# A two-layer graph kernel: tile 1 decoded by VectorE, GpSimd's work in other forms, the clip of the norm moved

## What is computed

```python
def _ngcf_conv(x, W1, W2, src, dst, n_nodes):
    deg_out = jnp.clip(segment_sum(ones, src), 1.0)
    deg_in = jnp.clip(segment_sum(ones, dst), 1.0)
    norm = jax.lax.rsqrt(deg_out[src] * deg_in[dst])
    h_src = x[src]
    h_dst = x[dst]
    msg = (h_src @ W1 + h_src * h_dst @ W2) * norm[:, None]
    agg = jax.ops.segment_sum(msg, dst, num_segments=n_nodes)
    return x @ W1 + agg

h = jnp.maximum(_layernorm(x, axis=-1), 0.0)
h = relu(_ngcf_conv(h, W1_1, W2_1, src, dst, n))
h = _ngcf_conv(h, W1_2, W2_2, src, dst, n)
return x + h
```

## Time and profile before

| | |
|---|---|
| median of three runs | 563.75 us (563.54 to 563.83) |
| the profiled execution | 563.75 us, of which the span is 559.7 us |
| PE, DVE busy in the span | 493.3 us (88%), 423.7 us (76%) |
| ACT, POOL busy in the span | 247.3 us (44%), 192.4 us (34%) |

### The profile page before, as it was taken

One profiled execution on the slowest core, in us unless ns is written; L12 is line 12 of the kernel. 1 busy time (PEld: TensorE's weight loads), 2 busy tenths in 40 slices (PEclk: granted clock), 3 DMA queues, 4 the chain that ended last, 5 costly groups with the idle time before them and its releaser, 6 DMA issues.

```text
span 559.7 us, 19159 instructions
## 1 busy us (share of the span) xinstructions
PE 493.3 (88%) x7774; PEld 457.8 (82%) x7774; DVE 423.7 (76%) x1157; ACT 247.3 (44%) x661; POOL 192.4 (34%) x307
## 2 busy tenths in 40 slices
PE   0294688899797999599999999999999999999995
PEld 0073577687586877499999999999899999999995
DVE  4698469999888798777887787788766666767673
ACT  0285488899796888523223222322211111111111
POOL 3679698879999998400000000000000000000000
PEclk9998699999989799889999999999999999999999
DMA  2166110000000000000000000000000020002011
GB/s 69 52 102 113 53 30 19 7 19 3 19 3 20 2 21 2 1 2 3 3 2 2 4 2 2 2 4 2 3 1 2 4 40 2 3 2 39 3 26 18
DMA packets 19428, 9.87 MB, mean 18 GB/s; under 512 B 16081, under 2 KB 18657, under 8 KB 19342
## 3 DMA queue, kind: packets, MB, share of 16 engines
q1 hardware_dynamic: 18222, 5.93, 5.9%
q0 software_dynamic: 1120, 2.72, 1.9%
HBM read 5.19 MB, written 1.65 MB: 12 GB/s over the span
## 4 chain that ended last, share of the span: by engine, by line
PE 35%; DVE 22%; POOL 12%; issue 10%; ACT 6%; SPq 2%; DMA 1%; DVEq 0%; ACTq 0%; POOLq 0%
PE diff L789 25%; DVE mixed L583 8%; PE slab L737 5%; ACT h L870 2%; POOL hist L394 2%; DVE work L667 2%; PE diff L773 2%; SPq L344 2%; DVE work L645 2%; PE diff L720 2%; DVE work L651 2%; DVE work L654 2%; POOL h L454 2%; POOL words L397 2%; DVE los L547 2%
## 5 line engine op out<-in xcount | busy, mean ns | idle before, releaser
L547 DVE TENSOR_TENSOR los<-mixed,iota_bank 128x6144 bf16<-128x6144 bf16 x49 | 161.9, 3344 | 10.9 <-PE slab L737 10.9
L789 PE MATMUL diff<-los,mixed 128*128 128x129 f16 x2401 | 159.7, 222 | 6.3 <-DVE los L626 5.7
L789 PEld LDWEIGHTS diff<-los,mixed 128*128 128x128 fp8e4 x2401 | 153.4, 101 | 8.3 <-issue 5.8
L789 PE MATMUL diff<-late,mixed 128*128 128x128 f16 x2401 | 150.7, 219 | 1.1 <-DVE late L670 1.1
L789 PEld LDWEIGHTS diff<-late,mixed 128*128 128x128 fp8e4 x2401 | 145.6, 98 | 2.0 <-DVE late L670 0.7
L737 PEld LDWEIGHTS slab<-hots,los 128*128 128x128 bf16 x2352 | 123.8, 101 | 22.0 <-ACT saved L831 8.4
L737 PE MATMUL slab<-hots,los 128*128 128x98 fp8e5 x2352 | 130.6, 213 | 4.6 <-DVE los L547 4.4
L823 ACT ACTIVATE hots<-diff 128x784 f16<-128x784 f32 x147 | 118.0, 843 | 18.7 <-PE diff L720 18.6
L720 PE MATMUL diff<-select,mixed 80*128 80x392 f16 x294 | 70.7, 345 | 30.3 <-DMA mixed<-rows 18.0
L583 DVE TENSOR_SCALAR mixed<-words 128x400 int32<-128x400 int32 x294 | 90.4, 363 | 0.0
L397 POOL COPY words<-saved 128x392 uint16<-128x392 uint16 x98 | 84.6, 864 | 0.0
(11 more groups left out here) (126 smaller groups left out, 370.4 us busy)
## 6 DMA issues: line engine op xcount, KB each, us to landing
mixed<-rows SPq DMA_DIRECT2D x147, 12.0 KB, 1.8
x_sb<-in_x_dram SPq DMA_DIRECT2D x4, 384.0 KB
out_dram<-x_sb SPq DMA_DIRECT2D x8, 128.0 KB
los<-in_dst_dram SPq DMA_DIRECT2D x1, 750.0 KB
out_dram<-x_sb SPq DMA_DIRECT2D x4, 80.0 KB
out_dram<-x_sb SPq DMA_DIRECT2D x4, 48.0 KB
los<-samples,row_i POOLq DMA_INDIRECT x7, 2.7
wt<-in_L_gnn_W_dram SPq DMA_DIRECT2D x4, 16.0 KB, 2.1
```

Source lines behind the costliest of these rows:

```text
L547: nc.vector.tensor_tensor(out=los[:, b % LOS_RING].rearrange("e s (v t) -> e s v t", t=2), in0=key, in1=val, op=ALU.is_equal).then_inc(los ...
L789: ins = nc.tensor.matmul(acc[a][:, 0:width], tiles[:, a, q], parts[:, q, 0:width], start=(q == 0), stop=(q == BLOCKS - 1))
```

## The change

VectorE's `decode_first` becomes `decode_early(t)` and is called for tile 1 as well, behind `low_hots(2)`. For tile 1 it waits for the lists (`fine_in`), for `turned`, and for all seven groups of DMAs of tile 0 (`stack_in`), since it writes the same `rows`. GpSimd's steps for tile 1, ScalarE's `save_source(1)` and VectorE's `weigh(1)` are gone; the turn and the keys of tile 1 come after units 3 and 4. `load_x` stands behind the rows of tile 1, and the stats begin at block 8. GpSimd's copy of words becomes a `tensor_scalar` with two operations, and so do its other forms with one. The norm is applied by one instruction for each block, 49 in all, after units 53 to 97 (`apply_norm`), without the clip. The clip is done twice, once inside the scaling on VectorE and once in place on `h[:, b]` by ScalarE in each position of layer 1. `unpack(1)` stands ahead of the wait for the histogram, and in unit 0 the weights beside it are made behind the products.

```diff
-    BEGIN = [max(0, UPT * t - 4) for t in range(TILES - 1)]
+    BEGIN = {t: UPT * (t - 1) - 4 for t in range(2, TILES)}
...
+    TURN_AFTER = {3: 1, **{u0 + 6: t for t, u0 in BEGIN.items()}}
+    KEYS_AFTER = {4: 1, **{u0 + 7: t for t, u0 in BEGIN.items()}}
...
-    STATS, PER_BLOCK = 6, 4
+    STATS, PER_BLOCK = 8, 4
+    MOMENTS = {44: 0, 45: 1, 46: 2}
+    STD_AFTER = 47
+    APPLY = 53
+
+    def applied(u):
+
+        return max(0, u + 1 - APPLY) * BLOCKS // (UNITS - APPLY)
...
-                if t == 0:
+                if t == 1:
                     load_x()
...
-                nc.gpsimd.tensor_copy(words[:, u // 2, 0:Q - 1, 8 * (u % 2):8 * (u % 2) + 8],
-                                      low[:, :, :, 0]).then_inc(words_copied, 1)
+                nc.gpsimd.tensor_scalar(words[:, u // 2, 0:Q - 1, 8 * (u % 2):8 * (u % 2) + 8], low[:, :, :, 0], 1.0, 0.0,
+                                        ALU.mult, ALU.add).then_inc(words_copied, 1)
...
-                    p(nc.gpsimd.tensor_scalar(p_i, q_i, -128.0, None, ALU.mult))
+                    p(nc.gpsimd.tensor_scalar(p_i, q_i, -128.0, 0.0, ALU.mult, ALU.add))
...
+            def apply_norm(b):
+                nc.gpsimd.tensor_scalar(h[:, b], x_sb[:, b], neg_mean[:, b:b + 1], rstd[:, b:b + 1],
+                                        ALU.add, ALU.mult).then_inc(normed, 1)
...
+                if u == APPLY:
+                    pool.wait_ge(rstd_ready, 1)
+                for b in range(applied(u - 1), applied(u)):
+                    apply_norm(b)
...
-            def decode_first():
-                sources, targets = fine[0][:, 0], fine[0][:, 1]
-                dve.wait_ge(fine_in[0], 32)
+            def decode_early(t):
+                sources, targets = fine[t][:, 0], fine[t][:, 1]
+                dve.wait_ge(fine_in[t], 32)
+                if t == 1:
+                    dve.wait_ge(turned, 1)
+                    for j in range(PER_TILE):
+                        dve.wait_ge(stack_in[0][j], 48)
...
+                if b == 2:
+                    decode_early(1)
...
             unpack(0)
+            unpack(1)
             dve.wait_ge(hist_added, UNITS + 1)
...
-            dve.wait_ge(words_copied, UNITS)
-            unpack(1)
...
-                nc.vector.tensor_tensor(out=scaled[:, qs], in0=h[:, qs],
-                                        in1=rdo_sc0[:, qs].unsqueeze(2).to_broadcast([128, PIECE, D]),
-                                        op=ALU.mult).then_inc(scaled_ready, 1)
+                nc.vector.scalar_tensor_tensor(scaled[:, qs], h[:, qs], 0.0,
+                                               rdo_sc0[:, qs].unsqueeze(2).to_broadcast([128, PIECE, D]),
+                                               ALU.max, ALU.mult).then_inc(scaled_ready, 1)
...
                     dve.wait_ge(root_ready, n + 1)
+                    dve.wait_ge(h_ready, n + 1)
...
+                    if n < BLOCKS:
+                        if n == 0:
+                            act.wait_ge(scaled_ready, BLOCKS // PIECE)
+                        act.wait_ge(normed, n + 1)
+                        nc.scalar.activation(h[:, b], h[:, b], ACT.Relu).then_inc(h_ready, 1)
                     act.wait_ge(acc_ready, n + 1)
```

More of the change, by code:

```diff
@@ L289, in fast_path @@
     POSITIONS = 2 * BLOCKS
[L291 to L296 removed]
+    BEGIN = {t: UPT * (t - 1) - 4 for t in range(2, TILES)}
+    DECODE = {u0 + after: (t, step) for t, u0 in BEGIN.items() for step, after in enumerate((0, 1, 2, 3, 4, 8, 9))}
+    WEIGH_BESIDE = {u0 // 2 + 4: t for t, u0 in BEGIN.items()}
+    SAVE_AFTER = {u0 + 4: t for t, u0 in BEGIN.items()}
+    TURN_AFTER = {3: 1, **{u0 + 6: t for t, u0 in BEGIN.items()}}
+    KEYS_AFTER = {4: 1, **{u0 + 7: t for t, u0 in BEGIN.items()}}
     FETCH_AFTER = {4 + 2 * (t - 2) + k: (t, k) for t in range(2, TILES) for k in range(2)}
     FIRST_SCALE, BOUND, SECOND_SCALE = 5, 12, 8
[L300 to L302 removed]
+    STATS, PER_BLOCK = 8, 4
[4 more added lines that the diff above has]
+        return max(0, u + 1 - APPLY) * BLOCKS // (UNITS - APPLY)
     STORES = ((0, 16), (16, 32), (32, 42), (42, 48), (48, 49))
@@ L413, in decode @@
                 elif step == 3:
-                    p(nc.gpsimd.tensor_scalar(q_rows[:], q_i, -float(MID), None, ALU.add))
+                    p(nc.gpsimd.tensor_scalar(q_rows[:], q_i, -float(MID), 1.0, ALU.add, ALU.mult))
                 elif step == 4:
@@ L423, in decode, with moments @@
                                             op=ALU.mult).then_inc(rows_ready, 1)
-            def norm_part(n):
+            def moments(n):
                 mean_e, mean_o = stats[:, :, 1], stats[:, :, 4]
@@ L725, in products @@
             def products(u):
-                for m in pairs_beside(u):
-                    weigh_hots(m)
                 if u >= 2:
@@ L746, in _ @@
             for u in range(UNITS):
+                if u > 0:
+                    for m in pairs_beside(u):
+                        weigh_hots(m)
                 products(u)
+                if u == 0:
+                    for m in pairs_beside(u):
+                        weigh_hots(m)
                 if u == BOUND:
```

47 lines of the change are left out of this document (13 added, 34 removed).

## The result

The changed kernel takes **559.58 us** (median of four runs, 558.20 to 560.32), the kernel before 563.79 in the same series: a ratio of 0.992 [0.989, 0.995] (in brackets the 95% interval, as everywhere below). It is faster by 4.2 us, where 11.2 were forecast. The profiled execution took 558.2 us, its span 556.5; it was the shortest of the four, 1.4 us under the median.

| | before | forecast | after |
|---|---|---|---|
| unit 18 starts | 76.6 | 69.0 | 73.2 |
| unit 18 to 40 | 41.6 | 42.6 | 42.4 |
| unit 40 to 97 | 109.7 | 98.1 | 101.3 |
| unit 97 to the first sums of layer 1 | 13.94 | 13.14 | 15.58 |
| layer 1 | 161.0 | 168.8 | 167.1 |

The account below looks back on a forecast made before the run. Waits and extra work, the largest PE's at unit 11, bound the build and a closed dependence ring layer 1; 563.75 - 18.2 (build) - 0.8 (step) + 7.8 (layer 1) = 552.55, said as 552.6 us, range 544 to 561.

Parts of the forecast that it names:

- the load of x: Start of the build: x issued from 52.2 us, behind 21 DMAs of rows, and there at 65.0.
- GpSimd keeps up: Units 40 to 97: GpSimd needs at most 1.4 of 1.62 us a unit, with words at 0.55.
- the new place of `unpack(1)`: Step to layer 1: `unpack(1)` behind `unpack(0)` is free and leaves the path to the reciprocal, 0.8 us less.
- start to unit 18: Start of the build: the 11.4 us stall at unit 11 goes, and unit 18 starts at 69.0 us.
- to unit 40: Units 18 to 40: VectorE bounds, with blocks with stats at 3.77 us each; forecast 42.6 us.
- to unit 97: Units 40 to 97: blocks at 3.25 us plus ScalarE's extra work and a wait, 98.1 us in all.
- the step: From unit 97 to the first sums of layer 1: 13.14 us, 0.8 us less than before.
- layer 1: The clip enters the dependence ring in 48 of 49 positions at 0.163 us each, 7.8 us more.
- outside the span: Part of the time outside the profiled span: forecast unchanged at 4.05 us.
- rival (a): Build: words stay at 0.86 us or GpSimd is late at the decodes; 3 to 4 us less gained, 556; chance 0.17.
- The root: Build, near unit 47: the moments come late, so ScalarE waits about 2 us before the root.
- Rival (b): Layer 1: the clip costs its whole length and a semaphore step, 14.6 us instead of 7.8, 559.4; chance 0.07.

Follow-up runs that it names:

- e7: Changed kernel with GpSimd's fetches for tiles 3 to 6 moved to units 14, 28, 42 and 56, those of tile 2 to units 1 and 2: 567.42 us.
- e2: Changed kernel with x loaded behind the rows of tile 0, as in the kernel before: 553.83 us.
- e9: Changed kernel with x behind the rows of tile 0 and the fetches of tiles 4 to 6 moved to units 20, 34 and 48: 550.82 us.
- d1: Changed kernel with the norm as in the kernel before, keeping the early decode, the order of x and the two-operation forms: 558.56 us.
- e4: Changed kernel without GpSimd's histogram addition in all units but the last, so its result differs: 552.87 us.
- e3: Changed kernel with GpSimd's words copied by the old plain copy: 558.67 us.
- e5: Kernel before with only GpSimd's instructions changed to the two-operation forms: 562.26 us.
- b3: e9 with the clip of h taken out of layer 1's positions and made by ScalarE in seven wide pieces in the step to layer 1: 545.96 us.
- b4: b3 with `unpack(1)` moved back behind the last histogram and the totals: 546.60 us.
- e1: Changed kernel without ScalarE's clip of h in layer 1 and VectorE's wait for it; the scaling still clips: 553.02 us.
- e8: Changed kernel with the fetches placed as in e7 and x issued behind the third group of rows of tile 1: 560.13 us.
- e10: e8 with GpSimd waiting before the words of units 16 and 30 until VectorE's first weigh step for tiles 2 and 3 is done: 555.63 us.

## Why the prediction was right and wrong

The direction was right, and the time lies in the range; but of the 11.2 us forecast only 4.2 came. Three steps failed: the load of x was taken to be 4.2 us shorter than it was, "GpSimd keeps up" did not hold (3.2 us net), and the new place of `unpack(1)` was not free (2.4 us). Two terms erred the other way and hid part of this. From 552.55 the terms missed by +4.2 (start to unit 18), -0.2 (to unit 40), +3.2 (to unit 97), +2.4 (the step), -1.7 (layer 1) and -2.35 (outside the span): together the profiled 558.2, but for rounding. The median is 1.4 us above this execution.

**The first unit 18: wrong by 4.2, all of it in x.** I had SP issue 21 DMAs of rows in 13.2 us and x from 52.2 on, landing 12 to 13 us later, at 65. The rows took 14.8 us, until 54.2, and x was there 14.9 us after that, at 69.16; from there to unit 18 it was 4.0 us, as forecast. Both were read from the kernel before, with two fetches beside each; here six stand beside the rows and four beside x. e7, with none and two, has 13.7 and 12.5. "VectorE and PE wait for x" was right as the wait that ended last, but not as the only one: I gave GpSimd's ten fetches no price, though they are issued between units 4 and 13, ahead of and between the first steps of the decode of tile 2. PE's idle time of 6.3 us at unit 16 was ended by ScalarE and, behind it, GpSimd, and 1.8 us were left at unit 18 of the forecast "6 us in its place at unit 18, ended by `los`". In the changed kernel this second wait cost nothing; it is what e2 ran into, and e9 shows it gone.

**Unit 18 to 40: right.** VectorE with its stats bounds, 42.4 against 42.6. But with x that late, the early decode as such gained little by then: unit 0 started 2.3 us earlier, and unit 40 was 2.6 earlier (0.9 in d1).

**"GpSimd keeps up": wrong, 3.2 us.** The price of the words was the named unknown, 0.55 from the row of the same opcode on another type. It was 0.875, as the copy had been: rival (a) held, with its 0.86. The histogram was put at 0.2, though its row has 0.294, and the narrow norm at 0.3; it took 0.42. These lengths overlap a little; from start to start a unit with one norm takes 1.45 us where I had 1.05. That still fits into 1.62. What does not fit is a unit with a step of the decode, 2.2 to 2.7 us: I had spread the decode evenly, 0.33 a unit, and an average hides it. The kernel before had shown the same already. I called its waits beside that at unit 11 small and named ScalarE's 3.06 us; from 118 to 228 us its view of waits has

```profile
DVE rows L536 <- POOL work L416: 9.2, 2, 5.3
```

and the changed kernel still has 6.3 of it. Rival (a) put 3 to 4 us on GpSimd's lateness, and 3.2 came; but this is a net figure. e4, with GpSimd relieved, takes 95.9 us, 2.2 under the forecast of 98.1: so the lateness cost up to 5.4, and the other terms were too dear by some 2. That (a) alone would give 556 was off by the other steps. e3 and e5 settle the form. The root waited 1.5 us, as forecast (2).

**The step to layer 1: wrong sign, 2.4 us.** "Its new place is free" was read from VectorE alone, which has nothing to do there. I did not ask who finishes the last histogram: GpSimd does, 4.4 us after the start of unit 97 instead of 1.9. b3 and b4 show that 0.9 of it is the stretching beside `unpack(1)`, which makes the new place a draw. The rest goes with the norm behind each of the last units, which come faster than GpSimd can serve them with it; d1, without it, has a step of 13.38.

**Layer 1: right mechanism, slightly too dear.** The distance behind the clip was 0.146 us, not 0.163, and a position grew by 0.144: 48 of them are 6.9. Against e1 the whole stretch is 7.2, by those of before 6.1. I had taken the row of L869, which writes another tile; the clip reads and writes the same one, and was shorter. The estimate beside it of 146 ns, from the Trainium skill, ScalarE: Activation LUTs, section What ACT_TABLE_LOAD costs, agrees with the trace, 0.146 us from the clip to its successor. PE's wait before each transpose came, in the row of its weight load, 0.15 us instead of the forecast 0.16. Rival (b), the whole length, did not hold.

```profile
311.97 0.14 PEld L770 LDWEIGHTS slab<-ident,work 128*128 128x128 f32 x1 [0.15 <-DVE work L659]
```

**Outside the span: no step at all.** I took the 4.05 us as constant. They fell by 2.35, and without that the change would be worth about 1.8 us. That the total came as near as it did is luck in this part: nothing in the prediction led to it.

## What to carry to other kernels

An average per unit does not tell whether an engine keeps up: GpSimd fits with 1.45 us of work into a slot of 1.62, but not with the 2.2 to 2.7 of the units with a decode step, and its lateness comes out again at the waits for that decode. Before calling a moved instruction free, look at the engine that works beside it, and before moving one wait away, list every queue that has grown in front of the next. Work that a ring of dependences must carry once per position is better done once, wide, outside it: here seven wide clips cost nothing visible in the span and 49 narrow ones 7 us. And compare two kernels by their spans, stretch by stretch, as well as by their times: here 2.4 us came and went outside the span.

## What was new about the hardware

- A VectorE instruction with two inputs from SBUF was held off by GpSimd over several instructions in a row: 4.10 us instead of 0.56 (e8, L538), 2.66 in e7, and 0.56 again once GpSimd paused (e10). The Trainium skill, SBUF — State Buffer, section Who interferes with whom, has the two engines share a pair of ports under an exclusive lock. The trace agrees that VectorE was held off, but the wait was longer than one instruction of the holder: in e8 VectorE did not get its turn between any of six. It need not last to the end of the stream: in e7 L538 got its turn behind the fourth, and the fifth lasted 0.57 us instead of 0.28.
- GpSimd's `tensor_scalar` with two operations instead of one took 510 to 520 ns instead of 1185 on 384 32-bit integers, made no difference on 392 16-bit words (875 in the changed kernel, 864 for the copy before), and was longer for a maximum on 448 fp32 columns (1709 in e5, 1325 before).
- The time outside the span followed VectorE's program: 3.9 to 5.0 us, or 1.7 to 2.2 with 48 or 49 instructions or waits more, in every execution of all twenty kernels; 16 more did not change it, nor did 49 on ScalarE.
